# Node stage of a graph kernel: a third half of node rows, a fourth of x, stores ahead of zeros, sums seven tiles later

## The reference

```python
neighbor_sum = segment_sum(x[col], row)
deg = max(segment_sum(1, row), 1)
mean_neighbor = neighbor_sum / deg
h_mean = (x + mean_neighbor) * 0.5 @ W_mean + b_mean
h_concat = concat([x @ W_ego + b_ego, mean_neighbor @ W_nb + b_nb])
gate = sigmoid(gate_weight * delta_agg + gate_bias)
x = layernorm(x + (1 - gate) * h_mean + gate * h_concat)
```

## Time and profile before

| | us |
|---|---|
| median of three runs | 2945.29 |
| lowest run | 2940.87 |
| profiled execution | 2944.66 |
| its span | 2942.9 |
| PE busy | 2697.9 (92%) |
| DVE busy | 2329.0 (79%) |
| ACT busy | 1851.3 (63%) |
| POOL busy | 1582.4 (54%) |

### The profile page before, as it was taken

The page is one execution under the profiler, slowest core; times in us unless marked ns, Lnnn a source line. Parts: engine busy times, 40 slices in busy tenths (PEclk is TensorE's granted clock), DMA queues, the critical chain, the costliest instruction groups (busy, mean ns, idle before and its releaser), DMA issues. The chain is left out here.

```text
span 2942.9 us, 52181 instructions
## 1 busy us (share of the span) xinstructions
PE 2697.9 (92%) x13617; PEld 1554.7 (53%) x13617; DVE 2329.0 (79%) x7668; ACT 1851.3 (63%) x3839; POOL 1582.4 (54%) x1491
## 2 busy tenths in 40 slices
PE   4789889999999959999999999999999999976774
PEld 2455556666666525555555555555555555543442
DVE  8777775655565668888888888888888888878996
ACT  2344445555555437777777777777777777757885
POOL 0476717676666375455455454454554554405776
PEclk8799999999999979999999999999999999999998
DMA  9999995565555478777777787777777777647994
GB/s 339 304 301 314 306 308 182 187 192 180 182 189 189 143 182 218 215 223 214 213 227 214 213 221 216 215 218 217 219 217 212 226 213 212 193 118 241 278 278 154
DMA packets 544632, 653.46 MB, mean 222 GB/s; under 512 B 244302, under 2 KB 451850, under 8 KB 544518
## 3 DMA queue, kind: packets, MB, share of 16 engines
q1 hardware_dynamic: 468486, 440.38, 51.6%
q0 software_dynamic: 69472, 208.99, 22.7%
q10 hardware_dynamic: 6560, 2.84, 0.4%
HBM read 315.65 MB, written 299.10 MB: 209 GB/s over the span
## 5 line engine op out<-in xcount | busy, mean ns | idle before, releaser
L942 PE MATMUL bank<-w_node,xT 128*128 128x384 f32 x1564 | 568.5, 501 | 47.2 <-ACT bank L576 46.9
L1219 ACT ACTIVATE hidT<-bank,b1c 128x512 f32<-128x512 f32 x490 | 336.8, 687 | 414.5 <-PE bank L1509 340.7
L1128 POOL TENSOR_TENSOR u_hc<-u_hc 128x1536 f32<-128x1536 f32 x98 | 270.2, 2757 | 551.0 <-issue 429.0
L1509 PE MATMUL bank<-xh,w1h 128*128 128x512 f16 x1568 | 469.8, 381 | 23.1 <-DMA xh<-eh 15.7
L1509 PE MATMUL bank<-xl,w1h 128*128 128x512 f16 x1568 | 468.2, 380 | 0.0
L1509 PE MATMUL bank<-xh,w1l 128*128 128x512 f16 x1568 | 468.2, 380 | 0.0
L942 PEld LDWEIGHTS bank<-w_node,xT 128*128 128x128 f32 x1564 | 291.4, 195 | 227.7 <-ACT bank L576 61.6
L576 ACT ACTIVATE bank<-bias_all 128x512 f32<-128x512 f32 x391 | 234.3, 599 | 267.4 <-DVE H L680 266.2
L1525 PE MATMUL bank<-hidT,w2f 128*64 128x256 f32 x3136 | 360.1, 382 | 0.8 <-ACT hidT L1219 0.8
L1350 DVE STREAM_TRANSPOSE feat<-catT 32x256 f32<-32x256 f32 x784 | 342.5, 437 | 17.0 <-ACT catT L1228 2.4
L673 DVE SCALAR_TENSOR_TENSOR H<-bank,gates,X 128x256 f32<-128x256 f32 x391 | 187.2, 479 | 175.1 <-PE bank L942 172.5
(11 more groups left out here) (248 smaller groups left out, 4833.0 us busy)
## 6 DMA issues: line engine op xcount, KB each, us to landing
hc_tab<-H SPq DMA_DIRECT2D x78, 680.0 KB, 7.9
er<-edge_tab SPq DMA_DIRECT2D x98, 512.0 KB
X<-in_x SPq DMA_DIRECT2D x78, 640.0 KB, 4.8
h_row<-hc_tab SPq DMA_DIRECT2D x97, 512.0 KB
out_x<-o_row SPq DMA_DIRECT2D x97, 512.0 KB, 5.0
hc_tab<-zero_row SPq DMA_DIRECT2D x35, 1344.0 KB, 8.4
edge_tab<-u_x SPq DMA_DIRECT2D x98, 256.0 KB
edge_tab<-feat SPq DMA_DIRECT2D x98, 256.0 KB
```

The source lines that it names most:

```text
L942: ins = t_.matmul(p[:, 0:384], xT[t // 2 % XR][:, t % 2, c * P:(c + 1) * P], w_node[:, c, :], start=False, stop=c == 1, skip_group_check=True)
L1128: g.tensor_tensor(c, c, u_hc[s][:, :, MULT:MULT + 3].unsqueeze(3).to_broadcast([P, 4, 3, P]), ALU.mult).then_inc(u_scaled, 1)
L1219: a.activation(hidT[m][:, :], bank[2 + m % 2][:, :], ACT.Relu, bias=b1c[:, m:m + 1])\
L1509: ins = t_.matmul(bank[2 + m % 2][:, :], w[:, c, m * P:(m + 1) * P], xx[s][:, :, :].rearrange("p (k c) e -> p c k e", c=2)[:, c, :, :], st ...
```

## The change

Four things: H has three buffers in rotation, not two, and the copy that opens a half waits for the store of three half rounds before. X has four buffers, not three, each loaded one half round further ahead. In each half round SP issues load, store, zeros, not load, zeros, store. The zeros after the first 144 tiles come in pieces of 6 and 7 tiles in turn, over 41 half rounds, not 7 tiles each over 38 and 1 tile in the 39th. The segment sums begin at tile 195, not 188, and are spread over 177 steps, not 186; FIX is one step earlier.

```diff
-        CLEARS = (0, 60, 88, 116) + tuple(range(144, NT, 7)) + (NT,)
+        CLEARS = (0, 60, 88, 116) + tuple(144 + 13 * c // 2 for c in range(38)) + (NT,)
-        XB = 3
+        XB = 4
-        H = [tmp(f"H{s}", [P, HALF, HU]) for s in range(2)]
+        HR = 3
+        H = [tmp(f"H{r}", [P, HALF, HU]) for r in range(HR)]
-        h_out = [sem(f"h_out{s}") for s in range(2)]
+        h_out = [sem(f"h_out{r}") for r in range(HR)]
-        SORT, PHASES, DECODE, SUMS, SPAN, FIX = 0, 7, 16, 188, 186, 378
+        SORT, PHASES, DECODE, SUMS, SPAN, FIX = 0, 7, 16, 195, 177, 377
...
-                def half(j, s):
-                    if 2 * j + s + XB <= 2 * ITER:
-                        load(2 * j + s + XB)
-                    if 2 * j + s < len(CLEARS) - 2:
-                        clear(2 * j + s + 1)
-                    store(j, s)
+                def half(h):
+                    if h + XB <= 2 * ITER:
+                        load(h + XB)
+                    store(h)
+                    if h < len(CLEARS) - 2:
+                        clear(h + 1)
...
                 def first(t, i):
-                    s, k = i // HALF, i % HALF
+                    h, k = t // HALF, t % HALF
+                    s = h % HR
                     dve.wait_ge(p_ready, t + 1)
-                    if t >= TEN and k == 0:
-                        dve.wait_ge(h_out[s], (t - i) // TEN * 16)
+                    if h >= HR and k == 0:
+                        dve.wait_ge(h_out[s], h // HR * 16)
```

More of the change, by code:

```diff
@@ L475, in load, with store @@
                         sp.dma_start(X[h % XB][:, 0, :], x[N - P:N]).then_inc(x_in[h % XB], 16)
[L477 to L480, removed]
+                def store(h):
+                    sp.wait_ge(h_done, (h + 1) * HALF)
+                    sp.dma_start(h_main[:, h * HALF:(h + 1) * HALF, :], H[h % HR][:, :, :]).then_inc(h_out[h % HR], 16)
                 def clear(c):
@@ L485, in clear @@
                                  zero_row[:, :].unsqueeze(1).to_broadcast([P, hi - lo, U])).then_inc(c_zeroed, 16)
-                def half(j, s):
-                    if 2 * j + s + XB <= 2 * ITER:
-                        load(2 * j + s + XB)
-                    if 2 * j + s < len(CLEARS) - 2:
-                        clear(2 * j + s + 1)
-                    store(j, s)
[L494 to L498, removed]
+                def half(h):
[4 more added lines that the diff above has]
+                        clear(h + 1)
+                for h in range(2 * ITER):
+                    half(h)
+                for r in range(HR):
+                    sp.wait_ge(h_out[r], 16 * len(range(r, 2 * ITER, HR)))
                 sp.wait_ge(h_done, NT + 1)
-                sp.dma_start(hc_tab[N - P:N, U:RU], H[0][:, 0, :]).then_inc(h_out[0], 16)
-                sp.wait_ge(h_out[0], 16 * ITER + 16)
+                r = 2 * ITER % HR
+                sp.dma_start(hc_tab[N - P:N, U:RU], H[r][:, 0, :]).then_inc(h_out[r], 16)
+                sp.wait_ge(h_out[r], 16 * len(range(r, 2 * ITER, HR)) + 16)
             @block.gpsimd
@@ L677, in add @@
                 def add(t, i):
-                    s, k = i // HALF, i % HALF
+                    s, k = t // HALF % HR, t % HALF
                     dve.wait_ge(a_done, t + 1)
@@ L885, in _ @@
                 hround = [0]
-                for s in range(2):
-                    v.memset(H[s][:, :, D + 3:HU], 0.0)
+                for r in range(HR):
+                    v.memset(H[r][:, :, D + 3:HU], 0.0)
                 def round_(j):
```

## The result

The changed kernel takes 2904.68 us (median of four runs, 2903.88 to 2906.18) against 2943.51 (four runs): the ratio is 0.987, with a 95% interval of 0.9854 to 0.9886. That is 38.8 us less. The forecast was 2929, its range ended at 2907, and rival (a), in which DMA stops being the bound, had said 2906. One of the four runs before took 7257.4 us and is no measure of the kernel; it is also one of the three behind the median of 2945.29 above. The other three have a median of 2941.73, 37.1 us above the changed kernel, and nine further runs of the kernel before had 2943.26, so the gain is 37 to 39 us.

The account below looks back on a forecast made before the run. It took nearly full DMA engines to bound the kernel before tile 188, PE after. Gains 16.4 + 10.5 less 10.3 and 1 gave 15.6 us, from 2944.7 to 2929.1; own range 2918 to 2937, 8 in 10 2907 to 2946.

Parts of the forecast that it names:

- rival (a): Before the sums, DMA stops being the bound and PE sets the pace: gain 38.7 us, so 2906; chance 0.13.
- Why the store is late: Half rounds before the sums: engines nearly full, store behind 1344 KB of zeros; more buffers win only the few per cent.
- part 2: Half rounds before the sums carry 6.5 tiles of zeros for 7, at 309 GB/s: 16.4 us gained.
- What bounds the kernel before tile 188: Before the sums, DMA is 0.95 to 0.99 busy; DVE waits 59.6 us for H stores and PE waits behind it.
- Part 1: Three H, four X, store ahead of zeros: half 3 ends at 117.1 us, not 119.99; fourth X worth 0.
- Part 3: Sums from tile 195 over 177 steps leave PE seven tiles less after their start: 10.5 us gained.
- Part 4: At pair 6 (tile 205), POOL's first put waits for later zeros and PE runs dry: cost 10.3 us.
- Clock: A PE hole of ten us lowers the granted clock and may cost 0 to 2 us; 1 us taken.
- (b): Before the sums, the DMA rate stays at 303 GB/s: gain 2.6 us, so 2942; chance 0.20.
- (c): Before the sums, SP's queue blocks and rounds stay at 9.00 us: a loss of 8.6, so 2953; chance 0.10.

Follow-up runs that it names:

- the one with the early ones: The changed kernel with the old table of zeros, the old sums (tile 188, 186 steps) and 16 fetches ahead of the first put, not 13: 2897.85 us, ratio 0.9841.
- the kernel with sevens and late sums: The changed kernel with the old table of zeros (7 tiles a half round), keeping the sums from tile 195 over 177 steps: 2897.14 us, ratio 0.9839.

## Why the prediction was wrong

The step that failed is in "Why the store is late" and part 2: "the engines are within a few per cent of full", "More buffers can win back only the few per cent", and with them the 309 GB/s. It read the DMA share of 0.99 at 310 GB/s as a limit. It is none: the engines gave 350 after, 362 when they were the bound, and up to 365 with the third H buffer alone. The share counts the time that packets are under way, not what moves. Two us at a time, the kernel before shows it within one round; loads were issued at 226.15, 234.98 and 243.67 us:

```profile
230.00:232.00 2.00, 0.89 (x5) 0.50 (x4) 1.97 (x8) 0.79 (x2) 1.39 (x3) 1.00 1.02 382
232.00:234.00 2.00, 2.00 (x7) 1.09 (x6) 1.80 (x7) 1.53 (x4) 1.70 (x2) 1.00 1.07 370
236.00:238.00 2.00, 2.00 (x10) 1.32 (x9) 0.21 (x2) 0.30 (x1) 1.53 (x2) 1.00 0.97 153
238.00:240.00 2.00, 1.20 (x4) 0.45 (x4) 1.97 (x11) 0.89 (x2) 1.56 (x2) 1.00 0.97 360
244.00:246.00 2.00, 2.00 (x11) 1.29 (x9) 0.36 (x1) 1.12 (x2) 1.39 (x3) 1.00 1.04 211
```

Shortly after a round is issued, 153 and 211 GB/s at a share of about 1; in the middle 360 to 382. After the change the stretches between 230 and 250 us move 326 to 380, and the lowest up to 260 us is 282. By the times of issue, only the tail of the old store and the beginning of the new load were under way at the round's turn. DVE waited for that tail (2.13 us, until 237.79 us), so the next round was issued late: a loop of latency in which the engines ran nearly dry once a round, not a lack of bandwidth. That either edit on the store ends it is shown; which transfer's packets the slow stretches hold, and why they count as under way so long, is not.

The prediction's table hid the same thing. Its row of 328 GB/s from 363 to 416 us is a mean; the kernel before, in two of its parts:

```profile
363.00:384.00 21.00, 16.91 (x67) 10.25 (x65) 11.94 (x43) 8.58 (x17) 11.40 (x13) 1.00 1.04 378
384.00:400.00 16.00, 13.89 (x49) 8.71 (x50) 13.37 (x48) 8.39 (x17) 0.00 (x0) 0.89 0.80 261
```

So "no stage of this trace reaches it", said of 358 GB/s and counted against rival (a), was true of the rows chosen and not of the trace.

Point by point:

- *What bounds the kernel before tile 188.* Right that PE waited for DVE and DVE for the store, and it named the zeros ahead of the store with one other buffer free. Wrong on the weight: it gave them only the few per cent and the rest to a limit. That all 59.6 us of waits would go, which it let stand only in part, is what the third H buffer alone did.
- *Part 1*, "the fourth X is worth 0": held in the changed kernel (2905.84 against 2904.68); where a round carries 7 tiles it is open. Half 3 was to end at 117.1 us and ended at 119.52 (its X load): DVE's 2.85 us for the store went to 0.45 for PE, but its wait for the sorted edges in the same half grew from 4.26 to 6.37 us. The third buffer and the order, which the sum gave hardly anything of their own, were each worth nearly the whole gain (40 and 39 us alone).
- *Part 2*, 16.4 us: measured 37.9. Rival (a) had 38.1. The lighter rounds, to which the prediction gave the gain, bring nothing that a run shows: with them and the late sums alone the kernel is 4.9 us slower.
- *Part 3*, 10.5 us: the work did move, but that is no gain of its own. Seven tiles cost PE the same ahead of the sums once PE is the bound there too. The kernel with the late sums and the one with the early ones, both without a hole, differ by 0.7 us (2897.14 and 2897.85). In the sum the 37.9 and the 10.5 are one thing: all the idle PE time that went.
- *Part 4*, 10.3 us: mechanism and place right, the size 5.36. The queue was empty at T (36 GB/s between 403 and 406 us), so the zeros landed 9.6 us after it and not 10.5; the fetch took 2.8 us, not 3.6; and PE had 9.5 us of work left, not 6.3.
- *Clock*, 1 us: hole and clock together were 7.8 us, so about 2.4. From 421 to 425 us the granted clock was 0.50, the lower of its two levels (1.2 GHz); it was back at 1.00 from 430 us on.
- *The rivals.* (a) is what happened, with 2906 against 2904.7, at a chance of 0.13. That its number is so close is partly luck: it began 2.4 us too early, took 7.65 us a half round where 7.55 were measured (3.5 us too much over 35), and had 9.9 us for hole and clock where 7.8 were lost. The 358 GB/s that the Trainium skill states (DMA: Bandwidth & Descriptors, Specifications) was the better guide than the row: 361 to 365 were measured over 60 us and more, and 378 over 21 us. (b) rested on the same misread share. (c) rested on SP's long issues. They cost nothing here: with the zeros ahead of the store and three H they stayed (12 us and more) at 2904.26 us, and in the kernel with sevens and late sums, where PE never waited, one load took 3.28 us to issue. Only with 9 tiles did they go with slower rounds.

The change as a whole: each of its two edits on the store brings nearly all of the gain by itself; its new table of zeros costs 6 to 8 us of it. The new table and the late sums hang together. With zeros until tile 204 the fetch behind the first put comes after tile 204, and sums from tile 188 would want it at tile 199; no run has that pair.

## What to carry to other kernels

A DMA share near 1 said here that something was always under way, not that the engines were full. Look at GB/s in stretches shorter than a loop round. Where it swings as here, between 150 and 380, the loop may be waiting for one transfer's latency, and one more buffer or an earlier place in the queue is worth trying by itself; here each won nearly all of it. To see the true ceiling, give the engines more than a round can carry (here 9 tiles for 7) and read the rate. When a bound goes, the next wait is usually one that had slack before: here the first put behind the last zeros, which three fetches more took away again.

## What the runs showed of the hardware beyond that

Writes of 1088 and 1536 byte rows beside reads of 5120 byte rows, with small gathers among them, ran at 357 to 365 GB/s on one core over stretches of 60 us (the runs with 7 or 9 tiles a round and either edit on the store), and at 370 to 383 from 363 to 384 us, when the small gathers had ended and the fetches of x ran (all kernels but the one with 9 tiles, whose zeros were over). With more outstanding than the engines could move, SP's issue itself took long: 5.03 us for a load that takes 0.35. And a hole of PE of 5.36 us was followed by transposes at half speed (1.12 us for 0.60), so that removing it gave back 7.8 us from the first sum to the end of the stage; behind the hole of 2.92 us in the kernel with the old table and the old sums they took 0.66, and removing that one gave back 3.1.
